# Group 0's adjacency as integers on the sync queue, and a new end on VectorE

## What is computed

```python
h    = x @ W_loop.T                                     # per graph, 128 x 128
g    = h @ Wg_loop.T
vals = (h + b_loop) * sigmoid(g + bg_loop)
x1   = layernorm(x + relu(adj_transposed @ vals))        # over the features
y    = (adj @ x1) @ L1_weight[0] + L1_bias
out  = layernorm(x1 + y)
```

## Time and profile before

| | us |
|---|---|
| median of 3 runs | 160.38 |
| lowest and highest of them | 160.07, 162.25 |
| the profiled execution's own time | 160.98 |
| its span, first to last instruction | 159.3 |
| PE busy | 148.5 (93% of the span) |
| DVE, ACT, POOL busy | 123.1, 123.7, 126.4 |
| mean granted clock of TensorE | 0.989 |

### The profile page before, as it was taken

How to read it: one execution, slowest core, us unless ns; L and a number is a source line. 1 busy time by engine, 2 the same in 40 slices (tenths; PEclk the granted TensorE clock), 3 DMA queues, 4 the chain that set the end, 5 groups by cost and what they waited for, 6 DMA issues and landing times.

```text
span 159.3 us, 3524 instructions
## 1 busy us (share of the span) xinstructions
PE 148.5 (93%) x1040; PEld 136.1 (85%) x1040; DVE 123.1 (77%) x322; ACT 123.7 (78%) x257; POOL 126.4 (79%) x197
## 2 busy tenths in 40 slices
PE   7599999999999999999999999999999999999910
PEld 3188899999999999999999999999999999999700
DVE  1239988898888888889888878888988888989960
ACT  3337676979799797979798897979797997769870
POOL 2052968797979979797979889797979799797960
PEclk9999999999999999999999999999999999999995
DMA  4999999969798997979697997979794929211053
GB/s 94 338 357 368 368 399 403 384 209 376 234 349 282 282 344 218 402 184 396 191 382 247 311 339 247 373 204 380 222 377 146 361 94 319 76 68 68 4 200 135
DMA packets 19605, 42.73 MB, mean 268 GB/s; under 512 B 2176, under 2 KB 3072, under 8 KB 19584
## 3 DMA queue, kind: packets, MB, share of 16 engines
q1 hardware_dynamic: 14256, 25.37, 47.2%
q0 software_dynamic: 4896, 16.78, 31.1%
q10 hardware_dynamic: 432, 0.33, 0.6%
HBM read 34.08 MB, written 8.39 MB: 267 GB/s over the span
## 4 chain that ended last, share of the span: by engine, by line
POOL 65%; issue 13%; PE 12%; DMA 4%; POOLq 1%; DVE 1%; ACT 1%; SPq 1%; DVEq 0%
POOL rstd L338 31%; POOL x L352 26%; PE hg_ps L428 7%; POOL adj_sb L325 4%; DMA xt_sb<-x_t_dram 4%; POOL adjt_sb L332 3%; PE loop_ps L444 2%; PE msg_ps L463 2%; PE y_ps L502 1%; POOLq L59 1%; POOL out_sb L363 1%; ACT out_sb L631 0%; DVE s_sb L818 0%; ACT gate L612 0%; POOLq L233 0%
## 5 line engine op out<-in xcount | busy, mean ns | idle before, releaser
L338 POOL TENSOR_TENSOR rstd<-var,power 128x8 f32<-128x8 f32 (+1 forms) x37 | 54.9, 1485 | 17.8 <-DVE var L797 17.7
L428 PE MATMUL hg_ps<-w_all,xt_sb 128*128 128x256 f32 x256 | 65.4, 380 | 1.7 <-DMA xt_sb<-x_t_dram 1.7
L352 POOL TENSOR_SCALAR x<-s_sb,mean_neg,rstd 128x128 f32<-128x128 f32 x120 | 52.2, 448 | 3.4
L428 PEld LDWEIGHTS hg_ps<-w_all,xt_sb 128*128 128x128 f32 x256 | 44.0, 191 | 6.0 <-issue 2.4
L631 ACT ACTIVATE out_sb<-z_sb,rstd 128x128 f32<-128x128 f32 x122 | 38.9, 390 | 1.3 <-POOL rstd L338 1.3
L810 DVE TENSOR_TENSOR vals<-hg_ps,gate 128x512 f32<-128x512 f32 x32 | 22.1, 690 | 20.9 <-ACT gate L612 20.8
L603 ACT ACTIVATE hg_ps<-gate_b 128x1024 f32<-128x1024 f32 (+1 forms) x32 | 31.8, 998 | 5.0 <-DVE vals L810 2.6
L444 PEld LDWEIGHTS loop_ps<-vals,adj_sb 128*128 128x128 f32 x256 | 33.3, 191 | 1.9 <-issue 0.4
L463 PEld LDWEIGHTS msg_ps<-adjt_sb,x 128*128 128x128 f32 x248 | 31.4, 191 | 3.1 <-issue 1.5
L444 PE MATMUL loop_ps<-vals,adj_sb 128*128 128x128 f32 x256 | 33.8, 275 | 0.1
L463 PE MATMUL msg_ps<-adjt_sb,x 128*128 128x128 f32 x248 | 33.2, 277 | 0.0
(11 more groups left out here) (63 smaller groups left out, 46.4 us busy)
## 6 DMA issues: line engine op xcount, KB each, us to landing
xt_sb<-x_t_dram SPq DMA_DIRECT2D x32, 256.0 KB, 4.9
x_sb<-x_dram SPq DMA_DIRECT2D x32, 256.0 KB, 3.8
out<-out_sb SPq DMA_DIRECT2D x31, 256.0 KB, 4.5
adj_sb<-adj_dram POOLq DMA_DIRECT2D x15, 512.0 KB, 5.1
adjt_sb<-adj_t_dram POOLq DMA_DIRECT2D x15, 512.0 KB, 6.1
adj_sb<-adj_dram POOLq DMA_DIRECT2D x2, 256.0 KB, 4.9
adjt_sb<-adj_t_dram POOLq DMA_DIRECT2D x2, 256.0 KB, 4.9
const_sb<-consts_dram SPq DMA_DIRECT2D x1, 192.0 KB, 5.7
```

The costliest lines, as they stand in the source:

```text
L338: nc.gpsimd.tensor_tensor(rstd[:, c % RSTD_RING, first:end, :].rearrange("p l b -> p (l b)"), var[:, c % 2, first:end, :].rearrange("p l b ...
L352: done = nc.gpsimd.tensor_scalar(x1[:, q % X1_RING, batch(b)], s_sb[:, q % S_RING, batch(b)], mean_neg[:, c % 2, b:b + 1], rstd[:, c % RST ...
L428: last = nc.tensor.matmul(hg_ps[:, q % 2, b, :], xt_sb[:, q % XT_RING, batch(b)], w_gate, start=False, stop=True, skip_group_check=True)
```

## The change

At the start, group 0's adjacency is no longer loaded by GpSimd but by SP, as integers, into a tile of its own (`first_edges`), directly behind x_t 0. VectorE waits for it ahead of `values(0)` and copies it into `adj_sb` as floats; TensorE's first `loop_sum` and ScalarE's `look(0)` wait for that copy (`first_floats`) instead of for the DMA.

At the end, GpSimd has no part in the second normalisation, and ScalarE does that of group 27 and of all graphs of groups 28 and 29. VectorE takes the variance of each half of the last group by itself (`last_variance`), GpSimd the root of each half by itself (`last_root`, two columns instead of four), and VectorE normalises all of group 30 and both halves of group 31 in three instructions (`last_norm2`). All of these are stored by SP: group 30, then each half of group 31; ScalarE issues no store.

```diff
--- before.py
+++ after.py
@@ -26,10 +26,10 @@
 ROOT1_LAG, ROOT2_LAG = 1, 4
 
 LAST = GROUPS - 1
-POOLED = GROUPS - 5
 ON_ACT = {GROUPS - 3: (2, 3), LAST: (0, 1)}
 
-TAIL = ((GROUPS - 1, 0), (GROUPS, 0), (GROUPS - 1, 1), (GROUPS, 1), (GROUPS + 1, 1), (GROUPS + 2, 1), (GROUPS + 3, 1))
+TAIL = ((GROUPS - 1, 0), (GROUPS, 0), (GROUPS - 1, 1), (GROUPS, 1), (GROUPS + 1, 1), (GROUPS + 2, 1), (GROUPS + 3, 1),
+        (GROUPS + 3, 2))
 FIRST = (0, 1)
 
 X_RING, XT_RING, ADJ_RING, S_RING, X1_RING, Z_RING, OUT_RING, RSTD_RING, STATS_RING = 6, 6, 4, 3, 5, 4, 8, 4, 4
@@ -72,6 +72,7 @@
         xt_sb = sb("xt_sb", [P, XT_RING, W], F32)
         adj_sb = sb("adj_sb", [P, 2 * ADJ_RING, W], F32)
         adjt_sb = sb("adjt_sb", [P, 2 * ADJ_RING, W], F32)
+        first_edges = sb("first_edges", [P, W], I32)
         gate = sb("gate", [P, 2, W], F32)
         vals = sb("vals", [P, 2, W], F32)
         s_sb = sb("s_sb", [P, S_RING, W], F32)
@@ -145,6 +146,7 @@
         w_gate_in = sem("w_gate_in")
         first_adj = sem("first_adj")
         first_adjt = sem("first_adjt")
+        first_floats = sem("first_floats")
         x1_dve = sem("x1_dve")
         consts_in = sem("consts_in")
         bias_in = sem("bias_in")
@@ -168,7 +170,6 @@
         var_done = sem("var_done")
         root_done = sem("root_done")
         nmr_done = sem("nmr_done")
-        out_pool = sem("out_pool")
         x1_act = sem("x1_act")
         x1_done = sem("x1_done")
         msg_done = sem("msg_done")
@@ -262,6 +263,7 @@
             sp.dma_start(wg_t[:, :], wg_loop_t).then_inc(fold_in, 16)
             sp.dma_start(w_all[:, P:2 * P], w_loop_t).then_inc(w_gate_in, 16)
             load_xt(0)
+            sp.dma_start(first_edges[:, :], adj[0, :, 0:W]).then_inc(first_adj, 16)
             load_xt(1)
             sp.dma_start(const_sb[:, :], consts).then_inc(consts_in, 16)
             load_x(0)
@@ -282,17 +284,16 @@
                 if exists(t - NORM2_LAG - 1):
                     sp.wait_ge(out_done, t - NORM2_LAG)
                     store(t - NORM2_LAG - 1)
-            sp.wait_ge(out_done, POOLED + 1)
-            sp.wait_ge(out_pool, 1)
-            store(POOLED)
-            for q in range(POOLED + 1, LAST):
+            for q in range(GROUPS - 5, GROUPS - 2):
                 sp.wait_ge(out_done, q + 1)
-                if q == LAST - 1:
-                    sp.wait_ge(out_dve, 1)
                 store(q)
-            sp.wait_ge(out_dve, 2)
-            sp.dma_start(out[LAST, :, 0:2 * P], out_sb[:, LAST % OUT_RING, 0:2 * P])\
-                .then_inc(out_st[LAST % OUT_RING], 16)
+            sp.wait_ge(out_dve, 1)
+            store(LAST - 1)
+            for p in range(2):
+                span = slice(2 * p * P, 2 * (p + 1) * P)
+                sp.wait_ge(out_dve, p + 2)
+                sp.dma_start(out[LAST, :, span], out_sb[:, LAST % OUT_RING, span])\
+                    .then_inc(out_st[LAST % OUT_RING], 16)
 
             def general_loads():
                 sp.dma_start(gw_t[:, :, :], w_rel_t).then_inc(gw_in, 16)
@@ -354,20 +355,14 @@
                         mean_neg[:, c % 2, b:b + 1], rstd[:, c % RSTD_RING, 0, b:b + 1], ALU.add, ALU.mult)
                 done.then_inc(x1_done, 1)
 
-            def pooled_norm2(q, graphs):
-                c = q + ROOT2_LAG
-                pool.wait_ge(root_done, root_count(c, 1))
-
-                pool.wait_ge(out_st[q % OUT_RING], 16 * (q // OUT_RING))
-                for b in graphs:
-                    done = nc.gpsimd.tensor_scalar(out_sb[:, q % OUT_RING, batch(b)], z_sb[:, q % Z_RING, batch(b)],
-                                                   rstd[:, c % RSTD_RING, 1, b:b + 1], zero[:, 0:1], ALU.mult, ALU.add)
-                if graphs[-1] == GB - 1:
-                    done.then_inc(out_pool, 1)
-
-
-            pool.wait_ge(warm_ready, 1)
-            pool.dma_start(adj_sb[:, 0, :], adj[0, :, 0:W]).then_inc(first_adj, 16)
+            def last_root(p):
+                c = LAST + ROOT2_LAG
+                pool.wait_ge(var_done, root_count(c, 1 + p))
+                pool.wait_ge(out_done, c - RSTD_RING - ROOT2_LAG + 1)
+                span = slice(2 * p, 2 * p + 2)
+                nc.gpsimd.tensor_tensor(rstd[:, c % RSTD_RING, 1, span], var[:, c % 2, 1, span], power[:, 1, span],
+                                        ALU.pow).then_inc(root_done, 1)
+
             pool.wait_ge(xt_in[0], 16)
             pool.dma_start(adj_sb[:, 1, :], adj[0, :, W:2 * W]).then_inc(adj_in[0], 16)
             pool.dma_start(adjt_sb[:, 0, :], adj_t[0, :, 0:W]).then_inc(first_adjt, 16)
@@ -389,10 +384,10 @@
             norm1(GROUPS - 1)
             roots(GROUPS - 1, 1, 2)
             roots(GROUPS, 1, 2)
-            pooled_norm2(POOLED, (2, 3))
             roots(GROUPS + 1, 1, 2)
             roots(GROUPS + 2, 1, 2)
-            roots(GROUPS + 3, 1, 2)
+            last_root(0)
+            last_root(1)
 
             def general_pair(pair):
                 pool.dma_start(adj_sb[:, 0:2, :], adj[bass.ds(pair, 1)].rearrange("o p (g n) -> p (o g) n", g=2))\
@@ -434,7 +429,7 @@
                 if exists(q):
                     spot = q // 2 % ADJ_RING * 2 + q % 2
                     if q == 0:
-                        pe.wait_ge(first_adj, 16)
+                        pe.wait_ge(first_floats, 1)
                     else:
                         pe.wait_ge(adj_in[q // 2 % ADJ_RING], arrived(q // 2, ADJ_RING))
                     pe.wait_ge(vals_done, q + 1)
@@ -630,7 +625,7 @@
                     for b in graphs:
                         last = nc.scalar.activation(out_sb[:, q % OUT_RING, batch(b)], z_sb[:, q % Z_RING, batch(b)],
                                                     ACT.Copy, scale=rstd[:, c % RSTD_RING, 1, b:b + 1])
-                    if not (q == POOLED + 1 and graphs[-1] == 1):
+                    if graphs[-1] == GB - 1:
                         last.then_inc(out_done, 1)
 
             def shared_norm1(q):
@@ -659,7 +654,7 @@
                 if 0 <= k < PAIRS:
                     spot = k % ADJ_RING
                     if k == 0:
-                        act.wait_ge(first_adj, 16)
+                        act.wait_ge(first_floats, 1)
                     act.wait_ge(adj_in[spot], arrived(k, ADJ_RING))
 
                     await_count(act, seen_done, k)
@@ -695,17 +690,12 @@
             look(PAIRS - 1)
             copy_messages(GROUPS - 2)
             shared_norm1(GROUPS - 1)
-            norm2(POOLED, (0, 1))
+            norm2(GROUPS - 5, (0, 1))
             copy_last_messages((0, 1))
-            norm2(GROUPS - 4, (0, 1))
+            norm2(GROUPS - 5, (2, 3))
             copy_last_messages((2, 3))
-            norm2(GROUPS - 4, (2, 3))
+            norm2(GROUPS - 4, every)
             norm2(GROUPS - 3, every)
-            norm2(GROUPS - 2, (0, 1))
-            norm2(LAST, (2, 3))
-            act.wait_ge(out_done, GROUPS)
-            act.dma_start(out[LAST, :, 2 * P:W], out_sb[:, LAST % OUT_RING, 2 * P:W])\
-                .then_inc(out_st[LAST % OUT_RING], 16)
 
             def copy_turned(step, ways):
                 act.wait_ge(rel_turned, step)
@@ -861,7 +851,6 @@
                     dve.wait_ge(x1_done, GROUPS)
 
                 dve.wait_ge(out_done, LAST - Z_RING + 1)
-                dve.wait_ge(out_pool, 1)
                 span = slice(2 * p * P, 2 * (p + 1) * P)
                 tt(z_sb[:, LAST % Z_RING, span], y_of(LAST, 2 * p)[:, span], x1[:, LAST % X1_RING, span], ALU.add)\
                     .then_inc(last_z_done, 1)
@@ -871,20 +860,28 @@
                 got = nc.vector.bn_stats(
                     stats[:, (LAST + ROOT2_LAG) % STATS_RING, 2 + p, :],
                     z_sb[:, LAST % Z_RING, 2 * p * P:2 * (p + 1) * P].rearrange("p (i n) -> p n i", i=2))
-                if p == 1:
-                    got.then_inc(bn2_done, 1)
-
-            def norm2_half(q, p):
+                got.then_inc(bn2_done, 1)
+
+            def last_variance(p):
+                c = LAST + ROOT2_LAG
+                dve.wait_ge(bn2_done, LAST + p + 1)
+                dve.wait_ge(root_done, root_count(c - 2, 1))
+                m2 = stats[:, c % STATS_RING, 2 + p, :].rearrange("p (i k) -> p i k", k=3)[:, :, 2]
+                ts(var[:, c % 2, 1, 2 * p:2 * p + 2], m2, 1.0 / P, EPS, ALU.mult, ALU.add).then_inc(var_done, 1)
+
+            def last_norm2(q, first, end, root):
                 c = q + ROOT2_LAG
-                dve.wait_ge(root_done, root_count(c, 1))
+                dve.wait_ge(root_done, root)
 
                 dve.wait_ge(out_st[q % OUT_RING], 16 * (q // OUT_RING))
-                span = slice(2 * p * P, 2 * (p + 1) * P)
-                tt(out_sb[:, q % OUT_RING, span].rearrange("p (b n) -> p b n", b=2),
-                   z_sb[:, q % Z_RING, span].rearrange("p (b n) -> p b n", b=2),
-                   rstd[:, c % RSTD_RING, 1, 2 * p:2 * p + 2][:, :, None].broadcast_to([P, 2, P]), ALU.mult)\
```

(13 more changed lines are left out.)

## The result

The changed kernel takes 158.87 us (median of 9 runs, 158.35 to 159.48) against 160.45 (9 runs, 159.97 to 162.25) for the kernel before, measured beside it: ratio 0.989, 95% interval 0.986 to 0.992. That is 1.6 us less, clear of the scatter and under the 2% that count as a change. The forecast was 159.0. The profiled execution took 159.41, its span is 157.7, again 1.7 apart; it is one of the two slowest of the nine.

What follows compares the result with a forecast made beforehand. The prediction took PE to bound the middle, so a start shift passes through. From the median of 160.38 us it took 1.4 (1.1 at the start, 0.3 at the end), giving 159.0, range 157.7 to 160.4.

Steps and rivals of the forecast that it cites:

- PE bounds the middle and a shift of the start goes through: Middle: PE-bound and the same in both kernels, 4.4 us per group; a start shift reaches the end one to one.
- The start, 1.1 us earlier: Start: first projection at about 6.5 instead of 7.62 us, 1.1 us earlier; ends of this term 0 and 1.73.
- x_t 0 lands near 6.1: Start: without GpSimd's packets, 1.28 us of engine time, x_t 0 lands near 6.1 instead of 7.37 us.
- the seed, at 6.42, is then last: Start: VectorE's seed, ending at 6.42 us, is the last thing the first projection waits for.
- x_t 1 just in time: Second projection: x_t 1, now behind the adjacency, lands near 7.8 to 8.2 us and is needed at 8.3.
- The cast costs nothing: VectorE ahead of `values(0)`: the integer-to-float copy, 0.69 us or half, fits in 3.82 us of idle time; cost 0.
- The third rival: Start: adjacency lands late and VectorE's wait holds `values(0)`; 161.1 us, or 160.8 with the end's gain; chance 0.06.
- The end, 0.3 us: End: rewritten normalisation and stores gain 0.3 us, between 0.15 by the drain and 1.2 by the landing.
- the term of the dispatch: End: VectorE's last instruction is dispatched at 154.25 instead of 154.40 us, a gain of 0.15 by the drain.
- The first: Start: x_t 0 is slow whoever stands beside it; start gains 0.2, total 159.9 us; chance 0.28 with the fourth.
- The second: Start and end: everything released, projection at 5.89 us, code fetch 0.9 earlier; total 157.75 us; chance 0.20.
- the fourth: End: three stores at 1.17 us issue each take back 0.2 to 1.4 us; 159.9; chance 0.28 with the first.

Runs made afterwards that it cites:

- e1: Kernel before with only the new start (SP loads group 0's adjacency behind x_t 0, VectorE copies it), old end kept: 159.18 us, ratio 0.986.
- e2: Changed kernel with the start edit undone, so the new end alone with the old start: 161.45 us, ratio 1.001 to the kernel before.
- e5: Changed kernel with group 0's adjacency loaded by GpSimd at the old place, as integers and copied by VectorE: 162.60 us in one run.
- e8: Kernel before with nine constant matmuls instead of five, filling PE's idle stretch ahead of the first projection: 160.42 us, ratio 0.998.
- e7: Changed kernel without VectorE's part of the general path, so without its flag load and jump: 158.05 us, ratio 0.980 to the kernel before.
- e9: Changed kernel with GpSimd waiting for its own last root before it loads the flag: 159.24 us, ratio 0.991 to the kernel before.
- e11: Changed kernel with GpSimd's flag load after its last root and VectorE's flag load ahead of its last instruction: 158.82 us, ratio 0.988.
- e3: Changed kernel with three constant matmuls instead of five ahead of the first projection: 159.07 us, ratio 0.985 to the kernel before.
- e12: Changed kernel unaltered, run again as the measure for later edits of the end: 159.32 us, ratio 0.990 to the kernel before.

## Why the prediction was right, and where it was not

- **PE bounds the middle and a shift of the start goes through.** Right: 140.5 us from first loop sum to last matmul against 140.65, while the loop sum came 1.4 us earlier.
- **The start, 1.1 us earlier.** Right in kind, too small: 1.4 in the profile, and e1 measures 1.9 us against the median of the kernel before beside it, with the low clock's part in it, and 1.6 against the median of that kernel's lower group (160.80). Two terms of the step were mis-sized. "x_t 0 lands near 6.1": it landed at 4.9, since the share of the engines' time that GpSimd's packets took (1.28 us) is less than what their being there cost (2.5). And "the seed, at 6.42, is then last": the gate bias lands after 2.5 to 3.0 us in every other profile here, with GpSimd's load in place too (e2, e5, e8); its 4.3 was peculiar to that one execution. So the seeds were over at 4.85, and the end of the constant matmuls, which I had as the far end of the range at 5.89, was the bound in this profile. Where PE speeds up sooner (e7, e9, e11) the start moves up to between 5.07 and 5.56.
- **x_t 1 just in time.** Half right: no wait in the two profiles of the changed kernel, but 0.2 to 0.7 us at the weight loads in four of the nine with this start. A wait there was one of the signs that the prediction gave for being wrong; it costs a part of the start's gain and not the gain.
- **The cast costs nothing.** Right: 0.43 us, nearer the lower of the two ends I gave, with 1.95 us of idle time behind it. The third rival did not occur.
- **The end, 0.3 us.** Too large: e2 shows no gain that can be measured, and the traces none at all. The fetch did gain, about 0.2 us: from flag load to drain it is 4.4 to 4.6 us in the three profiles with the old end and 4.1 to 4.4 in the eight with the new one. What failed is the term of the dispatch, "154.25 instead of 154.40". On the scale of before, the last root started at 153.55 and not at 153.44, and took 1.08 us and not 0.8, only 0.04 less than the one of four columns. So VectorE's last instruction was dispatched 0.2 us later, counted from the last matmul, and not 0.15 earlier; that used up what the fetch gained. Nor was there the 1.2 us by the landing: the last store was issued 0.7 us later from the last matmul than before and took 2.8 us, not 2.2. The reading that VectorE waits for its jump was right, as e7 shows, but the jump does not set the end alone; SP's wait for the last store ends within 0.3 us of it in six of the eight profiles. The Trainium skill (Runtime: NRT & Kernel Launch, "Instruction fetch mechanics") says that a taken branch to a page not held has to wait for a DMA fetch of it. The trace agrees: VectorE's drain comes up to 1.9 us behind the fetch in the changed kernel, and with the jump gone both the fetch and the wait are gone.
- **The rivals.** The first (x_t 0 slow for its own sake) is refuted by 3.1 us. The second had the start right, 5.89 with the load freed by more than its share; its end did not come. The Trainium skill (DMA: Bandwidth & Descriptors, "Latency and other measured facts") has two of the 16 DMA engines usually slower. Single DMA engines show in no row, so whether those two are what GpSimd's queue adds remains open. Of the fourth, one store's issue took 1.20 us and the two behind it 0.46 each. That put off the last store by 0.4 us (it is issued 4.0 us after the last matmul, in e3 3.6), which cost nothing in this profile, as VectorE's drain was later still:

```profile
152.57 1.20 SPq L261 DMA_DIRECT2D out<-out_sb  x1
```

The forecast of 159.0 met 158.87 partly by luck: 0.3 to 0.5 too little at the start and 0.3 too much at the end cancelled.

## What to carry to other kernels

Ahead of the first matmul order the loads by need in one queue: here a transfer that ran beside the first one cost it more than its bytes say, and one from GpSimd more still. Fill TensorE's wait ahead of its first real matmul, or better remove it: in a third of the runs the wait cost some 1.6 us over its own length. Before an end is rewritten for the sake of its last store, look at all the drains: what comes last may be a sequencer's jump, and where a jump and a landing end together, shortening one of them alone gains little.

## What was not expected

- PE's idle stretch of 1.7 to 2.1 us ahead of the first projection was followed by half the clock in e2 (0.50 from 8.5 to 11 us), and by full clock in the profile of before. It splits the times of one kernel into 160.1 to 161.1 and 162 to 163, with two single runs at 163.9 and 164.6; with the stretch filled (e8) the second group is gone.
- PEclk can read 1.00 while PE works at the lower rate: 512 columns per 0.43 us in the constant matmuls, and 16 projection matmuls in 4.4 us in e3 against 3.5 in e12.
- A jump of one engine over a long body takes some four microseconds from flag load to drain (4.1 to 4.6 in eleven profiles). With it gone (e7) the last store also landed 0.4 to 0.9 us sooner after its issue than in the other profiles with the new end, and the run was 1.0 us shorter than e3 and e1 beside it.
